# Attention: neighbouring blocks of exponentials are added before the product with ones, and constant rows are copied by transfers

## The reference

```python
key   = concat([ckv @ w_ku + b_ku, x @ w_kr + b_kr]); query = ...   # 16 heads of 32 columns
scores = einsum('bhqd,bhkd->bhqk', q, k)
scores = where(causal, scores, -inf)
at  = softmax(scores / sqrt(32), axis=-1)
out = einsum('bhqk,bhkd->bhqd', at, v) @ w_o + b_o
```

## Time and profile before

| | |
|---|---|
| median of 3 runs | 1191.31 us |
| profiled execution | 1188.85 us |
| its span | 1187.0 us |
| first attention core, from its first exponential | 418 to 586 us |
| second attention core | 680 to 849 us |
| TensorE busy over the span | 1048.3 us, 88% |
| VectorE busy | 883.8 us, 74% |
| ScalarE busy | 806.8 us, 68% |
| GpSimd busy | 373.1 us, 31% |
| mean granted clock of TensorE | 0.978 |

### The profile page before, as it was taken

How to read it: one execution, slowest core, us unless ns; L and a number is a source line. 1 busy time by engine, 2 the same in 40 slices (tenths; PEclk the granted TensorE clock), 3 DMA queues, 4 the chain that set the end, 5 groups by cost and what they waited for, 6 DMA issues and landing times.

```text
span 1187.0 us, 17822 instructions
## 1 busy us (share of the span) xinstructions
PE 1048.3 (88%) x5831; PEld 473.6 (40%) x5862; DVE 883.8 (74%) x2207; ACT 806.8 (68%) x1196; POOL 373.1 (31%) x409
## 2 busy tenths in 40 slices
PE   0787999988899789999999699999999799998786
PEld 0333455544454233233344233232344345554443
DVE  4778899999985787884334877884235799999893
ACT  5588898898644556567614465667547988899762
POOL 1122254454553040101210141002211144544456
PEclk9989999999999989999999899999999999999998
DMA  9555324332000145210001153110054333334000
GB/s 366 154 104 94 63 55 72 72 72 59 2 1 14 41 94 87 55 37 2 1 23 32 34 111 66 46 37 2 10 92 76 72 72 81 69 84 90 19 19 36
DMA packets 28969, 74.62 MB, mean 63 GB/s; under 512 B 5428, under 2 KB 7863, under 8 KB 24887
## 3 DMA queue, kind: packets, MB, share of 16 engines
q0 software_dynamic: 8320, 39.33, 18.3%
q1 hardware_dynamic: 20536, 33.99, 9.1%
HBM read 56.37 MB, written 4.21 MB: 51 GB/s over the span
## 4 chain that ended last, share of the span: by engine, by line
PE 58%; DVE 23%; issue 8%; ACT 4%; POOL 3%; DMA 2%; SPq 1%; DVEq 1%; another core or an unknown queue 0%; POOLq 0%; ACTq 0%
PE zP L560 12%; PE oP L608 9%; PE oP L729 5%; PE xP L729 5%; PE zP L713 5%; PE zP L655 4%; PE hP L692 3%; DVE arena L1368 3%; DVE m L1376 3%; PE zP L754 2%; PE hP L754 2%; PE hP L578 2%; DVE scored L1577 2%; PE zP L692 2%; PE zP L661 1%
## 5 line engine op out<-in xcount | busy, mean ns | idle before, releaser
L876 ACT ACTIVATE arena<-arena,X 128x2048 int8<-128x2048 f32 x154 | 307.8, 2005 | 7.4 <-DVE X L1348 6.2
L936 ACT ACTIVATE arena<-zP,asc 128x512 f32<-128x512 f32 (+3 forms) x384 | 200.6, 582 | 110.1 <-PE zP L717 80.7
L560 PE MATMUL zP<-T,arena 128*128 128x512 f16 x1024 | 243.7, 388 | 0.8
L608 PE MATMUL oP<-T,arena 128*128 128x512 f16 x832 | 199.2, 383 | 1.8 <-DVE arena L1463 1.8
L560 PEld LDWEIGHTS zP<-T,arena 128*128 128x128 f16 x1024 | 102.3, 100 | 122.7 <-issue 11.5
L832 ACT ACTIVATE arena<-zP,sc 128x512 f32<-128x512 f32 x128 | 87.2, 686 | 69.3 <-PE zP L560 69.0
L608 PEld LDWEIGHTS oP<-T,arena 128*128 128x128 f16 x832 | 81.3, 99 | 81.0 <-issue 6.8
L713 PE MATMUL zP<-arena 98*128 98x512 f16 (+3 forms) x384 | 110.4, 333 | 0.9 <-ACT arena L936 0.7
L1146 POOL TENSOR_TENSOR arena<-arena 128x512 f32<-128x512 f32 x16 | 20.3, 1270 | 256.2 <-DVE arena L1607 233.5
L1577 DVE CUSTOM_DVE_ANT_0 scored<-hP,causal 128x128 bf16<-128x128 f32 (+3 forms) x170 | 80.8, 484 | 21.6 <-PE hP L692 20.3
L692 PE MATMUL hP<-arena 96*128 96x512 f16 (+3 forms) x256 | 83.5, 345 | 14.8 <-DVE mx L1577 11.4
(11 more groups left out here) (205 smaller groups left out, 1774.0 us busy)
## 6 DMA issues: line engine op xcount, KB each, us to landing
arena<-bz_row POOLq DMA_DIRECT2D x26, 1024.0 KB, 8.3
arena<-arena SPq DMA_DIRECT2D x168, 64.0 KB, 2.0
arena<-bz_row POOLq DMA_DIRECT2D x6, 768.0 KB, 6.8
arena<-in_w_synT SPq DMA_DIRECT2D x4, 1024.0 KB, 8.1
arena<-in_w_outT SPq DMA_DIRECT2D x4, 1024.0 KB, 15.1
x_sb<-in_b_o POOLq DMA_DIRECT2D x2, 2048.0 KB, 19.0
out_dram<-x_sb SPq DMA_DIRECT2D x16, 256.0 KB, 2.0
x_sb<-in_x SPq DMA_DIRECT2D x3, 1024.0 KB, 13.9
```

Source lines behind the costliest of these rows:

```text
L560: mm = pe.matmul(zP[:, c * CW:(c + 1) * CW], part[:, g % 2, k, :], T1[:, k, c * CW:(c + 1) * CW], start=(n == 0 and k == 0), stop=(n == 1 ...
L608: mm = pe.matmul(o, part[:, k, :], T2[:, k, :], start=(c == 0 and n == 0 and k == 0), stop=False)
L876: act.activation(junk[:, counted[0] % 2, :], Z[:, g % ZR, :], ACT.Sign, bias=X[:, 2, k:k + 1], accum_out=S[:, k:k + 1]).then_inc(sm["cnt"], 1)
L936: act.activation(PT[:, m // 4 % 2, h, q0:512], colP[m % 3][:, q0:512], ACT.Exp, scale=asc[:, g, 10:11]).then_inc(sm["exp_done"], 1)
```

## The change

Neighbouring blocks of exponentials are added elementwise into `PS`, and one product with ones is done for the sum of the two. Pairs are blocks (0,1), (2,3), (4,5) of a unit with qc = 1 and (0,1) of a unit with qc = 0; unit (0,0) has none. Where the first block of a pair has 128 columns more than the second, those columns keep their own small product (`alone`). `add` stands behind the second block's `col` events, `sum` (the product with PS) behind head 0's `col` two blocks later. GpSimd does the additions of groups 0 to 2, VectorE those of group 3. ScalarE's exponential of head h, two blocks after the first of a pair, waits for that head's addition. GpSimd's normalization of the unit before now stands behind its additions of blocks (0,1) for qc = 0 and behind those of blocks (2,3) for qc = 1; in group 3 it keeps these places. PS takes the memory of `w_in`, which SyncE therefore loads again for b = 1 when the last product of core 0 is done. The constant rows of stacks 1 and 2 are no longer set by GpSimd but copied from stack 0 by SyncE, and the two memsets and their waits leave GpSimd's queue.

```diff
+def pairs(g, qc):
+    return () if (g, qc) == (0, 0) else ((0, P),) if qc == 0 else ((0, 0), (2, 0), (4, P))
+
+def alone(g, qc, kb):
+    q0 = max(0, kb * P - qc * 512)
+    for first, lo in pairs(g, qc):
+        if kb == first:
+            return (q0, lo) if lo else None
+        if kb == first + 1:
+            return None
+    return q0, 512
 def core_order():
             step = [("col", g, qc, kb, h) for h in range(HG)]
+            if kb - 1 in [first for first, lo in pairs(g, qc)]:
+                step.append(("add", g, qc, kb - 1))
+            if kb - 3 in [first for first, lo in pairs(g, qc)]:
+                step.insert(1, ("sum", g, qc, kb - 3))
...
-            passes = [{"col": 1, "norm": 0}.get(e[0], 3) for e in step]
+            passes = [{"col": 1, "norm": 0, "add": 0}.get(e[0], 3) for e in step]
+            for j, e in enumerate(step):
+                if e[0] == "mix" and alone(*e[1:]) is None:
+                    passes[j] = 0
...
+        PS = w_in.rearrange("p k n -> p (k n)").rearrange("p (h q) -> p h q", h=HG)
...
 SyncE
+                def unit_rows(g):
+                    eng.wait_ge(sm["unit_set"], 1)
+                    eng.dma_start(stacks[g][3 * HD:3 * HD + 2, 1, :, :], stacks[0][3 * HD:3 * HD + 2, 1, :, :])\
+                        .then_inc(sm[f"unit_in{g}"], 16)
                 load_stack(eng, b, 1, 0)
+                unit_rows(1)
                 max_rows(0, 1)
                 load_stack(eng, b, 2, 0)
                 max_rows(1, 0)
                 load_stack(eng, b, 2, 1)
+                unit_rows(2)
                 max_rows(1, 1)
...
                 if b == 0:
+                    eng.wait_ge(sm["mix_done"], TOTAL["mix"])
+                    load_w_in()
                     barrier(eng, 1 + b)
...
 TensorE
+                    elif kind == "sum":
+                        qc, kb = e[2:]
+                        lo = dict(pairs(g, qc))[kb]
+                        pe.wait_ge(sm["add_done"], HG * (m + 1))
+                        for h in range(HG):
+                            mm = pe.matmul(sumP[h * HD:(h + 1) * HD, lo:512], ones32, PS[:, h, lo:512],
+                                           start=(kb == 0), stop=False,
+                                           tile_position=(0, h * HD), skip_group_check=True)
+                        mm.then_inc(sm["sum_done"], 1)
...
 ScalarE, ahead of the exponential
+                        if kb - 2 in dict(pairs(g, qc)):
+                            act.wait_ge(sm["add_done"], HG * (n["add"] - 1) + h + 1)
...
 GpSimd
             def core(b):
-                for g in (1, 2):
-
-                    if g == 1:
-                        load_stack(pool, b, 1, 1)
-                        pool.wait_ge(sm["m_set"], b * TOTAL["max"] + 2)
-                    elif g == 2:
-                        wait_stack(pool, b, 0)
-                        wait_stack(pool, b, 1)
-                    unit_rows(b, g)
+                load_stack(pool, b, 1, 1)
                 pool.wait_ge(sm["a_xn"], (b + 1) * BT)
                 pool.dma_start(x_sb[:, b * BT:(b + 1) * BT, :], b_o...,
                                accum_op=ALU.add).then_inc(sm["bo_added"], 16)
...
+                for e in ORDER:
+                    if e[0] == "col":
+                        cols += 1
+                    elif e[0] == "add":
+                        g, qc, kb = e[1:]
+                        unit, lo = 2 * g + qc, dict(pairs(g, qc))[kb]
+                        if adds and g < GROUPS - 1:
+                            pool.wait_ge(sm["sum_done"], adds)
+                        for h in range(HG):
+                            if g < GROUPS - 1:
+                                pool.wait_ge(sm["exp_done"], cols - HG + h + 1)
+                                pool.tensor_tensor(PS[:, h, lo:512], PT[:, 0, h, lo:512], PT[:, 1, h, lo:512], ALU.add)\
+                                    .then_inc(sm["add_done"], 1)
+                        adds += 1
+                        if kb == (2 if qc else 0):
+                            attended(b, unit - 1)
...
 VectorE
+                    elif kind == "add" and g == GROUPS - 1:
+                        qc, kb = e[2:]
+                        lo = dict(pairs(g, qc))[kb]
+                        dve.wait_ge(sm["sum_done"], m)
+                        for h in range(HG):
+                            dve.wait_ge(sm["exp_done"], n["col"] - HG + h + 1)
+                            dve.tensor_tensor(PS[:, h, lo:512], PT[:, 0, h, lo:512], PT[:, 1, h, lo:512], ALU.add)\
+                                .then_inc(sm["add_done"], 1)
```

More of the change, by code:

```diff
@@ L117, in core_order @@
             step = [("col", g, qc, kb, h) for h in range(HG)]
+            if kb - 1 in [first for first, lo in pairs(g, qc)]:
+                step.append(("add", g, qc, kb - 1))
+            if kb - 3 in [first for first, lo in pairs(g, qc)]:
+                step.insert(1, ("sum", g, qc, kb - 3))
             if last:
-                step.insert(len(step) - MIX_LAG, ("mix_v", *last))
+                step.insert(step.index(("col", g, qc, kb, HG - MIX_LAG)), ("mix_v", *last))
                 step.append(("mix", *last))
@@ L327, in program @@
         COMPLETE = [max(n for n, e in enumerate(ITEMS) if plane(e) and plane(e)[1] == g) for g in range(GROUPS)]
-        TOTAL = {k: seen(k, len(ORDER)) for k in ("row", "max", "turn", "col", "mix", "norm", "rec", "mix_v")}
+        TOTAL = {k: seen(k, len(ORDER)) for k in ("row", "max", "turn", "col", "mix", "norm", "rec", "mix_v", "add", "sum")}
         RING = [e for e in ORDER if e[0] in ("row", "turn")]
@@ L476, in _, with load_w_in @@
             eng.wait_ge(sm["hT_ps"], 4 * 11)
-            for k in range(KD):
-                for w, lo in ((w_kv, 0), (w_q, 128), (w_kr, 256)):
-                    eng.dma_start(w_in[:, k, lo:lo + w.shape[1]], w[k * P:(k + 1) * P, :]).then_inc(sm["aw_in"], 16)
+            def load_w_in():
+                for k in range(KD):
+                    for w, lo in ((w_kv, 0), (w_q, 128), (w_kr, 256)):
+                        eng.dma_start(w_in[:, k, lo:lo + w.shape[1]], w[k * P:(k + 1) * P, :]).then_inc(sm["aw_in"], 16)
+            load_w_in()
             for b in range(2):
@@ L706, in core @@
                             pe.wait_ge(sm["mrow_in"], 16 * HG * (TOTAL["turn"] * b + 2 * g + qc + 1))
[L707 removed]
+                            if STACK_OF[g] == 0:
+                                pe.wait_ge(sm["unit_set"], 1)
+                            else:
+                                pe.wait_ge(sm[f"unit_in{g}"], 16 * (b + 1))
                             pe.wait_ge(sm["p_out"], (b + 1) * len(ITEMS))
@@ L1135, in core @@
                                accum_op=ALU.add).then_inc(sm["bo_added"], 16)
-                for m in range(TOTAL["norm"]):
-                    if b == 0 and m == TOTAL["norm"] - 1:
-                        rstd_rows(range(2))
-                    if b == 1 and m >= TOTAL["norm"] - 2:
-                        rstd1(1, m - TOTAL["norm"] + 2)
-                    g, qc = m // 2, m % 2
-                    a = attT[:, g, qc * 512:(qc + 1) * 512]
-                    pool.wait_ge(sm["mix_out"], b * TOTAL["norm"] + m + 1)
-                    pool.wait_ge(sm["rec_set"], 4 * (b * TOTAL["norm"] + m + 1))
-                    link(pool.tensor_tensor(a, a, rec_of(m), ALU.mult))
-                    pool.tensor_scalar(a, a, bcols[:, 10 + g:11 + g], None, ALU.add).then_inc(sm["attn_set"], 1)
+                cols, adds = b * TOTAL["col"], b * TOTAL["add"]
@@ new lines, in core @@
+                for e in ORDER:
[14 more added lines that the diff above has]
+                            attended(b, unit - 1)
+                        if b == 1 and kb == 0 and unit >= TOTAL["norm"] - 2:
+                            rstd1(1, unit - TOTAL["norm"] + 2)
@@ new lines, in core, with attended @@
+                if b == 0:
+                    rstd_rows(range(2))
+                attended(b, TOTAL["norm"] - 1)
+            def attended(b, m):
+                g, qc = m // 2, m % 2
+                a = attT[:, g, qc * 512:(qc + 1) * 512]
+                pool.wait_ge(sm["mix_out"], b * TOTAL["norm"] + m + 1)
+                pool.wait_ge(sm["rec_set"], 4 * (b * TOTAL["norm"] + m + 1))
+                link(pool.tensor_tensor(a, a, rec_of(m), ALU.mult))
+                pool.tensor_scalar(a, a, bcols[:, 10 + g:11 + g], None, ALU.add).then_inc(sm["attn_set"], 1)
```

30 lines of the change are left out of this document (17 added, 13 removed).

## The result

| | before | after |
|---|---|---|
| median | 1190.63 us (1188.03 to 1192.41) | 1215.64 us (1214.34 to 1219.63) |
| span of the profiled execution | 1187.0 us | 1217.8 us |
| mean granted clock of TensorE | 0.978 | 0.953 |
| TensorE busy over the span | 1048.3 us | 1055.3 us |

The ratio is 1.0215, with a 95% interval from 1.020 to 1.023: 25 us slower, where 2 us faster was forecast, and outside the range given.

A forecast was written before the change was run, and what follows sets the result against it. TensorE's queue was taken to set the pace. Each core: -12.4 us spared, +2.0 +0.3 +4.8 +1.4 +0.8 +2.0 of losses, -1.1; both -2.2, so 1189 us by the median, range 1173 to 1200.

The forecast's parts named there:

- TensorE's savings: Products with ones in each core: 6,784 fewer columns and 8 fewer groups spare TensorE 12.4 us.
- (0,1) first sum: Unit (0,1): TensorE waits for the first pair's additions before the product with their sum; loss 2.0 us (0 to 2.6).
- (2,1) first, third pair: Unit (2,1): first pair loses 0.3 us; third pair's additions, behind the normalization of (2,0), lose 4.8 (2.5 to 6).
- VectorE, turns: VectorE, 88% busy in (1,1), turns part of the gain into waits for row maxima: 1.4 us a core (0 to 3).
- b_o early: Block 0 of (0,1): b_o, issued earlier, lies across the small transfers of the maxima; 2.0 us stall (0 to 5.6).
- group 3: Units (3,0) and (3,1): ScalarE becomes the bound, so 0.8 us of the 3.3 us gain is lost (0.3 to 1.5).
- rival C: Clock: gaps from the (2,1) wait put 3 to 7 us of each core at half clock; 1192 to 1196, 14%.
- Rival B: Early b_o delays stack 1's last loads, group 1's row products and the maxima: 7.5 us a core, 1200 us, 14%.
- Rival A: Both cores: additions are in time, only VectorE, group 3 and b_o take from the gain; 1175 us, 32%.

The follow-up runs named there:

- experiment 7: Changed kernel with the b_o transfer and the normalization of (2,0) both moved behind the third pair's additions of (2,1): 1193.06 us, ratio 1.002.
- experiment 6: Changed kernel with GpSimd issuing the b_o transfer behind the third pair's additions in (2,1), not ahead of the core: 1203.22 us, ratio 1.0094.
- Experiment 5: Kernel before the change, with three extra VectorE reductions ahead of the maxima of unit (1,1), once per core: 1198.9 us, ratio 1.0056.
- experiment 1: Changed kernel without GpSimd's and VectorE's additions and the waits for them; order, early b_o transfer and constant rows stay: 1197.78 us, ratio 1.0056.
- first run of experiment 9: Changed kernel with b_o, normalization and reciprocals moved, plus row pace 5.7 for 5.5, moving 6 row products out of (1,1): 1182.39 us, ratio 0.9928.
- experiment 9: On the kernel with b_o, normalization, reciprocals moved: row pace 5.7, 1182.39 us; no additions in three units, 1178.24; both, 1179.65. Kernel before with reciprocals, pace moved: 1191.54.
- experiment 3: Changed kernel with GpSimd's normalization of (2,0) moved behind the third pair's additions in unit (2,1): 1203.15 us, ratio 1.0106.
- experiment 4: Changed kernel with 7 and 8 extra TensorE products ahead of its waits for row maxima at turns (1,1) and (2,0): 1219.33 us, ratio 1.0245.
- experiments 2: Changed kernel with GpSimd issuing the b_o transfer only when the maxima rows of (0,1) have landed: 1224.59 us, ratio 1.0297.

## Why the prediction was wrong

**TensorE's savings** are there, a little smaller than forecast. Products with ones stand in 40 groups a core. In group 3, where nothing else changed, (3,0) and (3,1) fell by 0.5 and 1.8 us in the first core and by 0.5 and 2.3 in the second; -3.3 + 0.8 = -2.5 was the forecast. (2,1) without its long wait (experiment 7) is 1.9 us shorter at 0.3 us more idle time: 2.1 us spared, where the sum had 2.6.

**The waits** were forecast at 11.3 us a core, and the idle time rose by 12.3. That the sum comes so near is partly luck, for terms too large and too small cancel:

```
                        forecast   measured, first core
(0,1) first sum            2.0      none (0.18 idle in all; 0.95 in the second core)
(2,1) first, third pair    5.1      4.35
VectorE, turns             1.4      1.16 + 2.07 + 1.23 = 4.5
b_o early                  2.0      3.8 (0,0)
group 3                    0.8      0.2
```

(2,1) is the forecast's chain link by link: reciprocals at 555.15, normalization at 558.68, additions at 561.57, and ScalarE's block 6 behind each of them:

```profile
562.68 0.47 ACT L991 ACTIVATE arena<-zP,asc 128x256 f32<-128x256 f32 x1 [3.09 <-POOL arena L1195]
```

The sum wait in (0,1) was hidden behind the stack's, and came, 1.0 us of it, when that was gone (experiment 6). GpSimd's additions took 1.24 and 0.96 us, where 1.3 and 1.0 were taken.

**The step that failed is the price of a wait.** The sum took each wait at its own length. The clock stood in rival C alone, tied to the wait in (2,1), with 3 to 7 us of low clock a core, 1.5 to 3.5 us lost, and 14%. Measured were 30 us of low clock a core more than before, and at 0.40 to 0.45 us for each 12 to 13 us lost: three to nine times the term. The mechanism was in the earlier trace rows, a stretch in which TensorE was busy for 0.78 us in 3 and had 0.50 after; what I had not done is ask that of every wait in the sum. Experiment 5 gives the factor at one place, 1.7 to 2. If all of the forecast's 11.3 us of waits are priced so, they are 19 to 23 us, less 12.4 spared: +7 to +10 a core, an estimate of 1205 to 1212. This would have been the right sign from the forecast's own terms. The factor is no constant: by the same account, with 0.40 to 0.45 us for each microsecond of low clock, it is 2.0 to 2.1 over both cores of the changed kernel, 1.6 to 1.7 without the additions (experiment 1), and 1.3 to 1.4 in the first run of experiment 9, whose 10.9 us more of idle time came with only 9.2 us more of low clock.

**The second mis-sized term** is VectorE's, 1.4 against 4.5 us. At the forecast's 25.81 busy of 29.3 us in (1,1) it has little to spare (measured were 26.66 of 33.10, waits and low clock in it), and its work isn't even: rows stand close ahead of a unit's turn, and there it is the bound. Ahead of the turns at 481.38 and 496.06 VectorE (the third of the busy times) has no gap, and what TensorE is spared, it waits:

```profile
476.00:478.00 2.00, 2.00 (x17) 0.54 (x14) 2.00 (x6) 1.70 (x4) 1.10 (x2) 1.00 0.01 4
478.00:480.00 2.00, 1.26 (x17) 0.51 (x13) 2.00 (x5) 0.58 (x1) 1.98 (x3) 1.00 0.00 0
...
494.00:496.00 2.00, 0.10 (x1) 0.00 (x0) 2.00 (x4) 0.30 (x1) 2.00 (x3) 1.00 0.04 8
```

Most of this term, 3.6 of the 4.5 us, is there without any addition (experiment 1), so it comes of TensorE having less to do. In experiment 9 the additions taken out of these three units made the kernel faster.

**Rival B** had the right mechanism, stack loads behind b_o's packets. The last load of stack 1, issued at 427.49, 1.3 us after b_o, landed at 434.14 (worked out from the trace). It took 6.65 us, where the last one took 2.3 in the kernel before, and group 1's first row product started at 434.23, behind the wait of 1.97 us. The wait of 2.32 us at block 0 of (0,1) is the one that the sum had, at 2.0. B's price in idle time, 7.5 us, was double the measured 3.8; taking the transfer away from there gave 12 us (experiment 6), the normalization of (2,0) another 12.5 (experiment 3). The two together bring the kernel back to the time before (experiment 7); what TensorE is spared beyond that went into the turns. **Rival A**'s 1175 is what the mended kernel comes near to: 1178.24, with three units' additions given up.

Two sums of the prediction are off by little and change nothing: the additions of (0,1) end at 445.5 by its numbers, not 445.6, and A's time with VectorE's loss left out is 1172, not 1173.

**What is not shown.** Why the same waits, 3.26 us in (1,1) of experiment 9 and 2.15 us in (2,0) of experiment 1, are followed by the low clock one time and not another. Whether products without use would hold the clock up (experiment 4 did not put them where TensorE stood). The 3.0 us more ahead of the first core in the changed kernel's profile: that part runs the same code, has 30.4 us of low clock where the profile before has 23.3, and in the other runs this lies between 13 and 31 for unchanged code.

## What to carry to other kernels

Take work from an engine only in stretches where it, and not the engine that feeds it, is the bound; elsewhere the saving comes back as waits. Price waits like these, 1 to 2.5 us on TensorE between busy stretches, at more than their length (1.3 to 2 times here), and look at the clock column behind each before the sum is made. When work is put into an idle engine's queue, list everything in that queue with its real length: here one normalization and one transfer's issue decided some 12 us each, and both could be moved to a gap.

## What the runs showed of the hardware

The issue of one 2 MB accumulating transfer shows as 1.67 us in GpSimd's timeline and held the engine for 12.5 to 13.5 us at one place of the core, and for 7.7 us at most at another (experiments 2, 7 and 9).

Two of VectorE's smallest operations took four and six times as long beside GpSimd's additions. The two that make the row maxima's halves take 0.18 us each in the run without additions. In the changed kernel, VectorE's timeline:

```profile
480.18 0.69 DVE L1662 TENSOR_SCALAR mrow<-mm_ 128x16 f16<-128x16 f32 x1
480.90 0.18 DVE L1663 SCALAR_TENSOR_TENSOR mrow<-mm_,mrow 128x16 f16<-128x16 f32 x1
...
493.24 0.18 DVE L1662 TENSOR_SCALAR mrow<-mm_ 128x16 f16<-128x16 f32 x1
493.45 1.14 DVE L1663 SCALAR_TENSOR_TENSOR mrow<-mm_,mrow 128x16 f16<-128x16 f32 x1
...
585.68 2.43 DVE L1641 TENSOR_TENSOR arena<-arena 128x512 f32<-128x512 f32 x4
...
589.87 3.99 DVE L1641 TENSOR_TENSOR arena<-arena 128x512 f32<-128x512 f32 x4
```

GpSimd's additions:

```profile
476.90 3.93 POOL L1195 TENSOR_TENSOR arena<-arena 128x384 f32<-128x384 f32 x4 [8.75 <-ACT arena L991]
...
493.30 3.71 POOL L1195 TENSOR_TENSOR arena<-arena 128x512 f32<-128x512 f32 x3 [6.24 <-ACT arena L991]
...
589.93 1.76 POOL L1211 TENSOR_TENSOR arena<-arena 128x512 f32<-128x512 f32 x1 [7.57 <-DVE arena L1680]
591.78 2.40 POOL L1212 TENSOR_SCALAR arena<-arena,bcols 128x512 f32<-128x512 f32 x1
```

Each slow operation ends about when one of these does: 480.87 beside 480.83, and 494.59 beside the first of three, 493.30 + 1.24. The last row's four additions stand beside GpSimd's normalization, whose two steps grew too, from 1.27 and 1.56 us to 1.76 and 2.40. The Trainium skill, "SBUF — State Buffer", in "Who interferes with whom", says that a VectorE instruction with two SBUF inputs contends with one of GpSimd's that reads SBUF, and that against VectorE in a two-port mode whoever issues first has the shared ports for the whole instruction while the other blocks. By that rule a 0.18 us operation may wait out a 1.24 us one, and these rows agree (0.69 and 1.14); which mode the first of the two ran in no run here shows. It is a small part here, 0.5 to 1 us ahead of a turn, but it falls on the path to a wait that is paid nearly twice.
